# TensorE's order in a step: the older unit's product ahead of the new unit's cosines

## What is computed

```python
# first layer, last part: rows of a message table gathered per edge, weighted, summed per destination
agg = segment_sum(messages[idx] * edge_weight, dst)
x = layernorm(x + agg + skip)
# second layer
Wh = x @ W + b
sim = dot(Wh[row], Wh[col]) / max(|Wh[row]| * |Wh[col]|, 1e-8)
out = scale * (c0 * segsum(base * relu(sim) * Wh[col]) - c1 * segsum(base * relu(-sim) * Wh[col]) + c2 * Wh)
x = layernorm(x + out)
```

## Time and profile before

| | us |
|---|---|
| median of three runs (lowest, highest) | 4669.24 (4663.32, 4670.95) |
| the profiled execution | 4667.63 |
| its span in the trace | 4666.1 |
| busy: TensorE, weight loads | 3164.4, 1891.2 |
| busy: VectorE, ScalarE, GpSimd | 3103.2, 1589.8, 3235.3 |
| mean granted TensorE clock (share of full) | 0.851 |

### The profile page before, as it was taken

How to read it: one execution, slowest core, us unless ns; L and a number is a source line. 1 busy time by engine, 2 the same in 40 slices (tenths; PEclk the granted TensorE clock), 3 DMA queues, 4 the chain that set the end, 5 groups by cost and what they waited for, 6 DMA issues and landing times. The chain is left out here.

```text
span 4666.1 us, 63774 instructions
## 1 busy us (share of the span) xinstructions
PE 3164.4 (68%) x16285; PEld 1891.2 (41%) x16285; DVE 3103.2 (67%) x5138; ACT 1589.8 (34%) x3302; POOL 3235.3 (69%) x3224
## 2 busy tenths in 40 slices
PE   4576777777767776776555555565477767677888
PEld 3344445444545444444334444443233232322222
DVE  6776767767776777774655555554377866576787
ACT  3422323223332323233421221221354544454444
POOL 0577777777777777775477777777576777776546
PEclk7888888888888889887777777777698989799899
DMA  3332323333332333232322222222355645455556
GB/s 63 120 93 91 100 87 98 91 91 98 94 97 89 98 90 99 89 98 83 111 72 66 79 70 66 81 68 67 112 159 147 175 133 159 122 156 152 174 172 194
DMA packets 355302, 502.08 MB, mean 108 GB/s; under 512 B 93127, under 2 KB 214984, under 8 KB 354809
## 3 DMA queue, kind: packets, MB, share of 16 engines
q1 hardware_dynamic: 251689, 394.52, 26.0%
q0 software_dynamic: 100352, 102.96, 10.7%
q10 hardware_dynamic: 2896, 0.59, 0.1%
HBM read 290.63 MB, written 207.16 MB: 107 GB/s over the span
## 5 line engine op out<-in xcount | busy, mean ns | idle before, releaser
L835 POOL DMA_INDIRECT frows<-messages,fidx x2352 | 2285.2, 972 | 831.5 <-issue 669.3
L915 PE MATMUL fps_b<-hot_key,hot_lo 128*128 128x343 f32 x3136 | 1235.0, 501 | 418.7 <-PEq L71 413.0
L974 DVE TENSOR_TENSOR strip<-strip,fps_b 128x343 f32 x1568 | 788.1, 503 | 541.6 <-DVEq L71 527.2
L850 ACT ACTIVATE turned<-fps_t 128x512 f32<-128x512 f32 (+1 forms) x754 | 431.9, 573 | 1750.9 <-ACTq L71 1748.0
L905 PE MATMUL fps_sum<-hot,frows 128*64 128x80 f32 x4704 | 550.0, 301 | 601.2 <-PEq L71 601.2
L1161 POOL DMA_INDIRECT lrows<-messages,lidx x784 | 744.6, 950 | 287.0 <-issue 221.6
L915 PEld LDWEIGHTS fps_b<-hot_key,hot_lo 128*128 128x128 f32 x3136 | 540.6, 206 | 743.2 <-issue 696.3
L905 PEld LDWEIGHTS fps_sum<-hot,frows 128*64 128x64 f32 x4704 | 521.9, 195 | 694.0 <-issue 694.0
L944 DVE TENSOR_SCALAR hot_key<-iota_f,edge 128x343 f32<-128x343 f32 x1574 | 753.4, 479 | 0.2
L1351 ACT ACTIVATE pos<-l_c,coeff 128x896 f32<-128x896 f32 x392 | 394.1, 1006 | 491.0 <-PE l_c L1222 490.2
L1222 PE MATMUL l_c<-unit_t,unit_g 64*128 64x448 f32 x1568 | 428.9, 624 | 159.3 <-DVE acc L1150 91.6
(11 more groups left out here) (192 smaller groups left out, 1983.4 us busy)
## 6 DMA issues: line engine op xcount, KB each, us to landing
adj<-turned SPq DMA_DIRECT2D x696, 256.0 KB
edge<-adj SPq DMA_DIRECT2D x294, 448.0 KB
adj_x<-adj SPq DMA_DIRECT2D x98, 448.0 KB
frows<-messages,fidx POOLq DMA_INDIRECT x2352, 2.4
messages<-msg SPq DMA_DIRECT2D x14, 1120.0 KB, 4.6
lrows<-messages,lidx POOLq DMA_INDIRECT x784
adj<-turned SPq DMA_DIRECT2D x58, 64.0 KB
wh_g<-wh_rows SPq DMA_DIRECT2D x56, 32.0 KB, 1.7
```

Of the source, the lines that this page charges most:

```text
L835: pool.indirect_dma_start(rows[:, q, k, :], None, tab_l[l].ap(), bass.IndirectOffsetOnAxis(ap=idx[:, q, k:k + 1], axis=0)).then_inc(s_got[ ...
L850: act.activation(turned[j][:, 0:(b - a) * P], ps_t[j][:, 0:(b - a) * P], ACT.Copy).then_inc(s_t_free, 1)
L915: pe.matmul(ps_b[n % KB][:, 0:NT * TWIN], hot_lo[:, s % 2, k, :], hot_key[:, n % KB, :], start=True, stop=True).then_inc(s_b, 1)
L974: dve.tensor_tensor(part, part, ps_b[n % KB][:, 0:NT * TWIN].rearrange("p (h w) -> p h w", w=TWIN), ALU.add).then_inc(v, 1)
```

## The change

```diff
                     for event in plan:
                         if event[0] == "unit":
                             u = event[1]
+                            if LAG <= u < len(units) + LAG:
+                                product(u - LAG)
                             if u < len(units):
                                 cosines(u)
-                            if LAG <= u < len(units) + LAG:
-                                product(u - LAG)
                         elif event[0] == "sum":
                             sum_row(event[1])
                         elif event[0] == "fin":
```

## The result

The changed kernel takes 4886.4 us (median of 4 runs, 4884.0 to 4890.0) against 4666.9 for the kernel before on the same chip (4663.3 to 4671.0): a ratio of 1.0468, with a 95% interval of 1.0455 to 1.0482. It is slower by 219.5 us. The forecast was slower by 110, so the sign was right, half of the size was missed, and the time lies above the range. The profiled execution took 4883.97 us.

The account below looks back on a forecast made before the run. TensorE was taken to bound the last part, GpSimd's gathers to set the first part's pace in the end. Profiled 4667.6 + 77 + 30 + 3 = 4778, so 4779 us against the median; range 4742 to 4812.

Parts of the forecast that it names:

- Part 1: Last stretch, units 256 to 391: products wait for VectorE's weighing, pairs take 5.21 instead of 3.71 us; 77 us in all.
- "out" periods: Ten-unit periods in the last part where VectorE's normalising holds the blend: 31.5 instead of 27.35 us each, 25 in all.
- Part 2: Units 0 to 50, ahead of row 14's gather: rows, visits and chunk turns delay the work by 30 us, bounds 11 and 45.
- The term of 0.90 a row: Rows of the first part: a product now stands between the sum and the next cosines, adding 0.90 us per row.
- Part 3: Units 51 to 255: GpSimd's 17.5 us a row sets the pace and buffer slack hides the lag; 3 us, bounds 0 and 20.
- The plain row: A row of five units without a visit, in the first part: 16.1 us, against GpSimd's 17.5.
- The row with a visit: A row of the first part with one visit and a quarter: about 18.0 us, against GpSimd's 17.5.
- The clock falls: Rival, last part: TensorE idles in every pair and drops to half clock, 6.85 us a pair, 4830 us; chance 0.04.
- The first part doesn't catch up: Rival: 20 us of lag stay until row 55, or half-clock waits double the early delay; about 4802 us, chance 0.12.
- Gathers hide the first part: Rival: VectorE's idle time absorbs nearly all delay up to row 10, row 14's gather starts as before; 4749 us, chance 0.20.
- one shift, no loop: Rival: the last part shifts once after each of seven refills, 4 us, rows may gain 10; 4663 us, chance 0.03.
- The mark of failure: The forecast is wrong if pairs take under 4.5 us or row 14's gather moves by less than 10 or over 50.

Follow-up runs that it names:

- filler: Changed kernel plus two matmuls computing nothing used on TensorE ahead of each row's sum; 4827.7 us, 59 less than the changed kernel.
- inplace_only: Against the kernel before: product-first order only up to unit 255, cosines first in the last part; 4801.7 us, ratio 1.0296.
- alone_only: Against the kernel before: product-first order only from unit 256 on, cosines first in units 0 to 255; 4753.9 us, ratio 1.0194.
- lag2_old: Kernel before, cosines first, with LAG 2 instead of 3, so the product behind cosines(u) is that of u-2; 4743.2 us, ratio 1.0164.
- filler_before: Kernel before plus one matmul computing nothing used ahead of each row's sum; 4669.6 us, ratio 0.9999.

## Why the prediction was half right

**Part 1 (77) held.** The stretch lost 82. The pairs are 5.21, the clock 1.00, and the waits end on VectorE's weighing, so the mechanism is the forecast one. With the 2.3 of the tail, 85 stand against 77. The term that was too small is that of the "out" periods, 25 for a measured 30.5: it had 4.1 for each (4.7 with the half clock that it mentions), and 4.6 and 5.5 were measured.

**Part 2 (30, bounds 11 to 45) held only at its bound.** The rows up to unit 50 lost 45, and row 14's gather came 42.6 later (30 forecast). The term of 0.90 a row fits: giving the cosines behind a sum their turn back brings 12.0 up to C50, where 11 sums stand (9.9 at 0.90), and 49 in all (55 rows at 0.90 are 50; the close fit is partly luck, since GpSimd's pace caps what a shorter row brings). The value of 30 left out more than one thing. It took every wait at full clock and kept half clock for the upper bound, but filler brings back only 6.5 up to C50; the visits given back bring 24.6, so the visits were the larger term that was too small.

**Part 3 (3, bounds 0 to 20) is the step that failed;** the stretch lost 89. Two terms of it were mis-sized. The plain row, 16.1, was right at full clock (15.94) but is 17.58 where the sum runs at half clock. The row with a visit was put at about 18.0 and took 21.97 and 22.68. So the mean row came to 18.8, over GpSimd's 17.5, and the argument of the slack turned round: four buffers hide a lag that GpSimd's pace catches up, and here the rows themselves had become the slower side, so that the loss ran on to the end. GpSimd's wait for a free buffer, which Part 3 put at nothing behind row 14, came back at 16 rows. The experiments put sizes to it, as differences of the first part from before (134 after): filler leaves 79, the visits given back leave 62, both together leave 20. In filler the stretch C50 to C119 is 241.8, that is 17.5 a row, and GpSimd goes at 17.85; only with the visits given back as well does it go at its 17.52 without a wait. So both terms had to be right for Part 3's argument to hold.

**The sentence behind the half clock** is in Part 2: "The product that leaves the end of the row (3594.30) was hidden: [...] so it gives nothing back." As a matter of turns that is true, the sum starts no earlier. But the hidden product was what kept TensorE's idle time ahead of the sum at 1.01. Without it the idle time is 1.91, and of 56 sums 34 run at half clock, not 13. I had costed an edit at nothing and not asked what the cover does to the clock when it is gone.

**The rivals.** "The clock falls" was right in kind and wrong in place. I put it into the last part, since TensorE idles in each pair there, and there it stays full. It fell in the first part. The section of the Trainium skill that I named ("TensorE: Matmul & The Clock Gate", "HAM oscillation — how this bites in real kernels") says that idle gaps in a repeated loop can throw TensorE back to half clock in each turn: by that rule, the trace agrees in part for the rows (0.87, sums of 3.61, but in 34 of 56 rows and not in each), and not for the pairs (1.00 at gaps of 1.35). "The first part doesn't catch up" (4802, 0.12) is the nearest to what happened; its two causes, the lag that stays and waits at half clock, were both there, and not as one or the other, so that the time lies 84 above it. "Gathers hide the first part" and "one shift, no loop" are ruled out by inplace_only (+137) and alone_only (+89).

**The mark of failure** that I set, pairs under 4.5 or row 14's gather outside 10 to 50, did not catch the miss. Both held, and neither looks at rows behind row 14. A mark on the mean row length, which I gave for a plain row alone, would have.

## What to carry to other kernels

Swapping two steps in an in-order queue does two things, to be priced apart: it takes one turn off the lag of the moved step (in plain pairs lag2_old takes the same 5.21 us as the swap), and it changes what stands beside each odd event between the steps, here sums, visits and turns (134 us at three places in the first part, at most 8 elsewhere there). When a step that was hidden in front of a wait moves away, don't cost it at nothing: look in the trace at how long the instructions take that stand behind a longer idle time of that engine. And where slack is to absorb a delay, compare the two paces first: slack absorbs a lag, not a slower pace.

## What the runs showed of the hardware

- The same idle time of 1.91 ahead of a sum went once with a sum at half clock (3.61) and once at full clock (2.05). The row with the half clock came behind an idle time of 1.63 ahead of the cosines at 3640.06 and the other behind 1.64 at 3781.89, so the waits of the row itself don't tell them apart; what does stays open. As a share: 13 of 56 sums are slow at a mean idle time of 1.03, 34 at 2.06, 6 at 0.57. But filler_before has 10 at 0.36, so the idle time ahead of the sum doesn't set the share alone.
- Idle time of 1.35 in each pair, 74% busy, left the clock at 1.00 through 109 us. So mean busy share doesn't tell of the clock: the rows were 74% busy too, at 0.87.
- Two matmuls that compute nothing, put where TensorE waits, made the kernel 59 us faster than the same order without them, and one made no difference in the kernel before, where the wait was 1.03.
- The first step of the normalising on VectorE (L1457, 128x448) took 2.50 beside 2.0 us of GpSimd's weighing and 1.45 beside 1.0 us of it, six times each. GpSimd as the cause was not tried apart.
